# A decoder layer on one core: one wait on the load queue, another PSUM bank for two weight transposes, and five re-ordered steps of the input quantisation

## The reference, cut to what matters

```python
x = x + attention(layernorm(x))                  # own keys, softmax over keys, two cells masked to -1e9
x = x + cross_attention(layernorm(x), ctx, mask) # K, V from ctx; softmax(energy, axis=1): over the HEADS
x = x + ffn(layernorm(x))                        # gate, up (256->1024), down (1024->256)

def fake_quant_nvfp4(x, global_scale):           # per block of 16: e4m3 scale, e2m1 values
    amax = max(abs(xb), axis=-1)
    sc8  = clip(amax / 6 * global_scale, 0, 448).astype(e4m3)
    dq   = sc8 / global_scale
    a    = clip(abs(xb) / dq, 0, 6)
    q    = sign(xb) * FP4_VALS[digitize(a, FP4_MIDS)]
    return q * dq
```

## Time and profile before

| | us |
|---|---|
| median of three runs | 632.37 |
| the profiled execution | 634.35 |
| its span in the trace | 632.3 |
| self attention, and the change of block | about 0 to 170 |
| cross attention, passes 0 to 15 | about 177 to 505 |
| feed-forward loop | about 505 to 632 |

### The profile page before, as it was taken

The page is one execution under the profiler, slowest core; times in us unless marked ns, Lnnn a source line. Parts: engine busy times, 40 slices in busy tenths (PEclk is TensorE's granted clock), DMA queues, the critical chain, the costliest instruction groups (busy, mean ns, idle before and its releaser), DMA issues.

```text
span 632.3 us, 14568 instructions
## 1 busy us (share of the span) xinstructions
PE 522.1 (83%) x6000; PEld 378.5 (60%) x6000; DVE 519.0 (82%) x660; ACT 332.9 (53%) x563; POOL 359.3 (57%) x295
## 2 busy tenths in 40 slices
PE   4799999997488999999999998998999664645544
PEld 4677777775356777767676676666776432323332
DVE  3587888888666788788899898888899889999996
ACT  2566766664153655556664575456554442625332
POOL 6401332232315776768858868777867768585540
PEclk9899999999697999999999999999999795778766
DMA  8900000000010011101111011101100000000000
GB/s 200 302 36 2 2 2 3 2 2 2 9 58 6 2 43 43 39 11 41 43 43 34 11 43 43 45 3 42 45 8 9 1 9 7 4 14 18 17 33 33
DMA packets 16644, 20.75 MB, mean 33 GB/s; under 512 B 2822, under 2 KB 14323, under 8 KB 16579
## 3 DMA queue, kind: packets, MB, share of 16 engines
q1 hardware_dynamic: 14658, 19.04, 10.0%
q10 hardware_dynamic: 1920, 0.79, 0.6%
HBM read 16.16 MB, written 1.84 MB: 28 GB/s over the span
## 4 chain that ended last, share of the span: by engine, by line
DVE 30%; PE 25%; POOL 12%; issue 4%; ACT 1%; DVEq 0%; POOLq 0%
DVE negmax L796 11%; POOL work L1214 6%; PE scores L1339 5%; PE head_out L1377 5%; PE scores L1349 4%; DVE den L804 4%; PE wide L1441 3%; DVE x_r L862 2%; DVE rden L809 2%; PE head_out L1365 2%; DVE work L903 1%; PE small L1463 1%; DVE unit L890 1%; POOL qv L1271 1%; DVE work L899 1%
## 5 line engine op out<-in xcount | busy, mean ns | idle before, releaser
L1214 POOL TENSOR_TENSOR work<-work,rden 125x1792 f32<-125x1792 f32 x48 | 172.3, 3589 | 3.8
L1040 ACT ACTIVATE work<-scores 125x896 f32<-125x896 f32 x96 | 88.7, 980 | 99.5 <-PE scores L1349 98.2
L796 DVE TENSOR_REDUCE negmax<-scores 125x112 bf16<-125x1792 f32 x48 | 97.2, 2025 | 33.5 <-PE scores L1339 33.0
L804 DVE TENSOR_REDUCE den<-work 125x56 f32<-125x896 f32 x96 | 101.9, 1062 | 10.3 <-ACT work L1040 9.9
L1212 POOL TENSOR_TENSOR rden<-rden,stays 125x112 f32<-125x112 f32 x48 | 20.5, 427 | 89.7 <-DVE rden L809 89.7
L1349 PE MATMUL scores<-negmax,identb 125*125 125x448 bf16 x192 | 46.5, 364 | 18.1 <-DVE negmax L796 15.6
L311 DVE TENSOR_REDUCE a_mpad<-a_s_ps 112x8 bf16<-112x896 f32 x32 | 33.5, 1093 | 24.3 <-PE a_s_ps L485 21.2
L1339 PE MATMUL scores<-qz,kT 32*125 32x224 f32 x768 | 51.2, 382 | 1.2 <-DVE gateT L791 0.8
L1377 PE MATMUL head_out<-work,v 125*32 125x112 f32 x1536 | 49.9, 270 | 2.1 <-POOL work L1214 2.1
L1441 PE MATMUL wide<-ctxT,ck 128*128 128x375 f32 x128 | 49.7, 513 | 0.0
L1506 PE MATMUL wide<-identb,qv 128*128 128x128 bf16 x112 | 14.1, 304 | 42.2 <-POOL qv L1271 34.5
(11 more groups left out here) (220 smaller groups left out, 1207.5 us busy)
## 6 DMA issues: line engine op xcount, KB each, us to landing
ctx_sb<-in_ctx SPq DMA_DIRECT2D x16, 375.0 KB
mask_sb<-in_mask_Bx1xSxS_if SPq DMA_DIRECT2D x16, 164.1 KB, 5.5
xsx<-in_x SPq DMA_DIRECT2D x4, 448.0 KB, 9.1
out_x<-ores SPq DMA_DIRECT2D x6, 256.0 KB, 2.1
a_raw_w<-in_L_ffn_gate_w SPq DMA_DIRECT2D x1, 1024.0 KB, 6.2
a_raw_w<-in_L_ffn_up_w SPq DMA_DIRECT2D x1, 1024.0 KB, 8.7
a_raw_w<-in_L_ffn_down_w SPq DMA_DIRECT2D x1, 1024.0 KB, 10.7
xt<-xsx SPq DMA_DIRECT2D x4, 112.0 KB, 2.2
```

Source lines behind the costliest of these rows:

```text
L796: dve.tensor_reduce(negmax[0:KP, :], scores[0:KP, :, 0:4 * TOK].rearrange("p j (h t) -> p t j h", h=4), AX.XY, ALU.max, negate=True).then_ ...
L804: link(dve.tensor_reduce(den[0:KP, kc, half], ex2[0:KP, kc, :, half, :].rearrange("p g t s -> p t g s"), AX.XY, ALU.add))
L1040: act.activation(ex2[0:KP, kc, 4 * i:4 * i + 4].rearrange("p (j m) t s -> p j m s t", m=NE), scores[0:KP, 2 * i:2 * i + 2, 0:4 * TOK].rear ...
L1214: pool.tensor_tensor(ex2[0:KP, kc], ex2[0:KP, kc], over, ALU.mult).then_inc(s["prob"], 1)
```

## The change

On the load queue of the first block a wait for the first of the `max` counts is put ahead of the first context load:

```diff
+                sp.wait_ge(s["max"], 1)
                 for b in range(2):
                     load_context(sp, b, b)
                     load_mask(sp, b, b)
```

The third weight half goes through `small` instead of `head_out`, and the halves 2 to 5 are spread over passes 0 to 3, one each, all at the place that halves 3 to 5 had. VectorE copies them at the place that halves 2 and 3 had:

```diff
-            return (scores[:, 0], head_out[:], head_out[:], small[:], small[:], small[:])[i].bitcast(BF16)
+            return (scores[:, 0], head_out[:], small[:], small[:], small[:], small[:])[i].bitcast(BF16)
...
-                        if b == 0:
-                            pe.wait_ge(s["w_sb"], 3)
+                        if b == 0:
+                            pe.wait_ge(s["w_sb"], 2)
...
                 def weight_T(i):
-                    if i == 2:
-                        pe.wait_ge(s["w_sb"], 2)
-                        pe.wait_ge(s["gone_read"], 2)
-                    if i >= 3:
+                    if i >= 2:
                         small_free()
                         pieces_read.n = i + 1
...
                         key(new, 0, 0)
-                    if n == 0:
-                        weight_T(2)
                     if now:
                         score(now, 2)
...
                         key(new, 1, 1)
-                    if n == 0:
-                        weight_T(3)
-                    if n in (1, 2):
-                        weight_T(n + 3)
+                    if 0 <= n < 4:
+                        weight_T(n + 2)
```

On VectorE `x_shifted` moves from behind `key_max` of chunk 1 to behind `inverse` of chunk 2 of the old batch, and `x_inverse` from behind `key_max` of chunk 1 to behind `x_variance`, near the end of the pass:

```diff
                     if old:
                         head_sum(old, 2, 1)
                         inverse(old, 2)
+                    if fourth is not None:
+                        x_shifted(fourth)
...
                         x_block_max(second)
-                    if third is not None:
-                        x_inverse(third)
-                    if fourth is not None:
-                        x_shifted(fourth)
                     if now:
                         head_sum(now, 0, 1)
                         inverse(now, 0)
                         head_sum(now, 1, 0)
                         key_max(now, 2)
-                    if n == 0:
-                        weight_piece(2)
-                        weight_piece(3)
-                    if n in (1, 2):
-                        weight_piece(n + 3)
+                    if 0 <= n < 4:
+                        weight_piece(n + 2)
                     if first is not None:
                         x_statistics(first)
                         x_variance(first)
+                    if third is not None:
+                        x_inverse(third)
                     if fourth is not None:
                         x_rounded(fourth)
```

On ScalarE `x_magnitude` moves from the middle of one pass to the start of the next, and for pair 4 behind the second input copy of the feed-forward part:

```diff
-                    second, third = pair_begun(n - 1), pair_begun(n - 2)
+                    second, fourth = pair_begun(n - 1), pair_begun(n - 3)
+                    if fourth is not None:
+                        x_magnitude(fourth)
                     if now:
                         half_exp(now, 0, 0)
...
                         flat_values(now)
-                    if third is not None:
-                        x_magnitude(third)
...
                 input_T_copy(1)
+                x_magnitude(NPT - 3)
```

On GpSimd `x_scales` moves behind `normalise` of chunk 2 of the old batch, and `x_units` behind `own_queries` and `output_bias`:

```diff
                     if earliest is not None:
                         x_product(earliest)
-                    if earlier is not None:
-                        x_scales(earlier)
                     if old:
                         normalise(old, 2)
                     if earlier is not None:
-                        x_units(earlier)
+                        x_scales(earlier)
                     if now:
                         normalise(now, 0)
                     if new:
                         own_queries(new)
                         output_bias(new)
+                    if earlier is not None:
+                        x_units(earlier)
                     if now:
                         normalise(now, 1)
```

## The result

The changed kernel took 625.14 us (median of 4 runs, 621.93 to 627.40), the kernel before, run beside it, 633.12 us (4 runs, 630.69 to 634.58). The ratio is 0.9865 with an interval of 0.9821 to 0.9909. The profiled execution took 627.4 us, of which the trace spans 625.5; before it was 634.35 and 632.3.

What follows compares the result with a forecast made beforehand. No single engine bounds it: PE and DVE are both busy 82 to 83%, and cross attention is a ring of dependent steps. 5.5 - 0.1 + 2.06 + 1.55 + 0.45 = 9.5 us off 632.37 gives 622.9 us; range 619.5 to 628.

Steps and rivals of the forecast that it cites:

- The weight strand: Pass 0: mask-copy wait and one weight transposition removed from before the scores of chunk 2; 5.5 us gained.
- The copy from pass 1: Pass 0's new timing taken from the same sequence in pass 1: scores of pass 1 at 194.85 instead of 200.35.
- The rival of a slow clock: Pass 0: PE stays at the lower clock, so 5.5 us becomes 2.8; time 625.6 us, chance 0.13.
- The weight half in pass 3: Pass 3 gets one transposition and a copy it did not have; cost 0.1 us, at most 1.01.
- The context loads: Four load DMAs wait 1.7 us for the first maximum; taken as 0, at most 0.5 us gain or loss.
- The GpSimd order: Passes 8, 10, 15: seven small POOL operations no longer precede normalise(old, 2); PE's waits for L1214 go, 2.06 us gained.
- x_shifted: Moved right behind the inverse, with POOL idle, taking 0.68 us: 1.55 us off passes 8, 10, 15, and 0.45 after pass 11.
- x_inverse: This 0.34 us DVE step moves to a place with 0.3 to 0.4 us of idle DVE time; cost 0.
- nothing comes of it: ScalarE or the query operand replaces pass 0's wait and the rest cancels: 631 to 633 us, chance 0.04.
- only the weight strand pays: x_shifted and the GpSimd order change who waits, not when a pass ends: 627.0 us, chance 0.13.
- `x_shifted` loses the race: Passes 7, 9, 11, 14: POOL issues first and DVE stands until L1214 ends; slower, 638.2 us, chance 0.04.
- PE stays fast at the end of pass 15: Clock stays high there: 0.7 us for head outputs and 0.6 for scores gained on top; 621.6 us, chance 0.13.

Runs made afterwards that it cites:

- the experiment that keeps the wait: Changed kernel with TensorE's wait for ScalarE's mask copy put back ahead of the scores of chunk 2 in pass 0, without the transposition: 631.01 us.
- the kernel of the input steps alone: Kernel before with only the order of the quantisation steps changed, without the load wait and the weight transposes' edits: 629.65 us, ratio 0.9949.
- the later comparison: Unaltered changed kernel timed again, beside the one with x_shift behind the last half sum of chunk 2: 625.23 us, ratio 0.9871; the other 621.65 us, 0.9818.

## Why the prediction was right, and where it was not

*The weight strand: right, in place and size.* Forecast 5.5 us, measured 5.53. That the two meet so closely is in part luck: against the three executions with the old order it is 4.2 to 5.6. The copy from pass 1 carried over to the instruction: from the scores of chunk 2 to those of pass 1 it said 5.95 us, and it is 5.99 (191.15 to 197.14). PE stands still for 0.69 us, where 0.7 was said. The rival of a slow clock (2.8 us, not 5.5) falls; the experiment that keeps the wait shows that its mechanism is real, and comes with the wait: 2.65 us of idle time, and then 1.64 us lost at a low clock.

*The weight half in pass 3: right.* 0.1 forecast, 0.10 measured.

*The context loads: right as far as it can be told.* The kernel with that edit alone shows no change, in an interval from 0.6 us faster to 2.6 us slower; the 0.5 us that were allowed can't be tested by it. The 2.3 us by which pass 0 began later in the profiled execution are not from it. Ten profiled executions with the wait begin pass 0 at 174.1 to 179.8 us, four without it at 174.3 to 180.0, and the changed kernel alone at 179.68 and 174.06.

*The GpSimd order: nearly right.* All three waits of PE for POOL are gone. The kernel with `x_shifted` at its old place against the kernel before shows -0.48 and -0.67 us for passes 7 to 10 and -0.64 for 14 and 15: 1.8 us, of the 2.06 forecast. The missing part sits in passes 7, 9 and 14, which grew by 0.27, 0.09 and 0.11 in that kernel; the paragraph on `x_inverse` says why. `x_magnitude` at 0 was right: in pass 11 it takes 0.62 us, and ScalarE still stands idle for 4.10 us behind it.

*x_shifted: right in sum, wrong in place.* Forecast 1.55 + 0.45 = 2.0 us, measured 2.0. L857 takes 0.63 us, where I took 0.68. The row that I read for it was not one with POOL idle: L1263 of POOL began at 518.37, just behind L856 at 518.35, and took 2.45 us. But I had the late start of passes 8, 10 and 15 shrink from 1.09 to 0.6 us. It vanished, and passes 7, 9 and 14 became 0.6 to 0.8 us longer instead. The prediction said itself that the maximum of chunk 1 would come 0.6 us later, and took that as hidden. It is, alone: where `x_shift` doesn't wait, passes 7, 9 and 14 are 19.6 us long with `x_shifted` at the new place. It is not on top of the wait of 0.81 us that `x_shift` puts ahead of the same maximum. The prediction never named that wait. It said that DVE has no idle time in passes 7, 9 and 14, and that reading was wrong: the trace of before has DVE idle there for 0.54, 0.68 and 0.62 us ahead of `x_shift`. In passes 11 and 12 the gain was 0.68 instead of 0.45 us, which hid part of what was missing elsewhere.

*x_inverse: wrong at 0.* I put it at 0 because it moved to a place with 0.3 to 0.4 us of idle DVE time. That place is ahead of the inverse for which GpSimd waits, GpSimd's normalisation stands ahead of `x_deviation`, and VectorE asks for `x_deviation` at the start of the next pass with nothing left to do meanwhile. In the kernel with only `x_shifted` put back passes 7, 9 and 14 came out 0.27, 0.09 and 0.11 us longer, 0.47 in all, and 0.36 of it came back in the kernel with `x_inverse` ahead of `key_max` of chunk 2: 0.14 of the 0.27 in pass 7, where the other 0.13 lies in `x_variance`, held up beside GpSimd. The rest of the 1.0 us that this kernel gains lies in passes 6, 8, 10, 11 and 13, in which the changed kernel lost nothing by the move of `x_inverse` (pass 6 is 19.64 and pass 11 19.96 us, before 19.62 and 19.96): it is a gain that the forecast did not claim, and no part of its shortfall.

*The shortfall.* Passes 7 to 15 gave 3.5 us of the 4.1 forecast in the profiled execution. In three more kernels in which these passes have the same order they gave 3.9, 3.9 and 3.2, and 3.0 in the second profiled execution of the changed kernel. The spread comes from the end of pass 15, where the clock differs.

*The rivals.* That nothing comes of it falls with the interval of the result, which ends at 0.9909. That only the weight strand pays (627.0) falls with the kernel of the input steps alone, 0.9949 with an interval below 1. That `x_shifted` loses the race doesn't happen at this place. One half sum later it does: passes 7 to 12, 14 and 15 of that kernel are 13.9 us longer than before, where the working, with GpSimd's gain of 2.06 taken off, had 11.2; it left out the clock behind the wait. Its time of 638.2 us met a measured 640.0. PE stays fast at the end of pass 15: not in the changed kernel (1.72 us), but in two of its variants, for 0.8 us instead of the 1.3 allowed, and for 0.4 to 1.2 us against the other executions with the same steps. Which of the two comes in a given execution no run settles.

*The rest.* Between the first and the last score group the change gave 8.9 us of the 9.5 forecast. By the medians it gave 8.0 us (633.12 to 625.14) and, in the later comparison, 8.8 (634.04 to 625.23). The forecast of 622.9 us had been counted from 632.37, the median of the first three runs; 0.8 of the 2.2 us between it and 625.14 is that the runs beside the changed kernel had a median of 633.12.

## What to carry to other kernels

When a step is moved into a gap of its own engine, follow the next result of that engine which another one waits for, and on to where that one's answer is wanted back: a gap ahead of a handover is not free. A step that waits for another engine should have one step of its own engine put ahead of it; here this, one half sum, was worth about as much as the move of the five steps (3.9 us against 3.5 by the passes, 3.6 against 3.2 by the medians and ratios). And a long wait of TensorE is priced with the slow instructions behind it, where the clock falls: here these came to 1.5 and 1.6 us on top of 3.1 and 2.0.

## What the runs showed of the hardware

*The start of pass 0 scatters by 6 us,* from 174.1 to 180.0, and by 5.6 us between two executions of the changed kernel itself, 179.68 and 174.06. It goes with TensorE's granted clock early on. The stretch from 22 to 35 us of the two executions, first that with the late start; the third figure from the end is the clock:

```profile
22.00:35.00 13.00, 11.15 (x125) 8.80 (x123) 6.21 (x13) 6.90 (x19) 3.01 (x4) 0.74 0.81 250
```

```profile
22.00:35.00 13.00, 10.87 (x174) 8.40 (x167) 11.18 (x19) 6.83 (x17) 3.66 (x5) 1.00 0.76 242
```

TensorE did 174 matrix multiplications in the one and 125 in the other in the same time, and VectorE had 11.18 us of work instead of 6.21. Over all fourteen profiled executions it is the same: with a granted clock of 1.00 in this stretch pass 0 began at 174.1 to 176.1 us (five), with 0.87 at 175.1 to 177.4 (three, the kernel before among them), with 0.74 at 178.8 to 180.0 (six). What decides it, no run here tells; it is why a single profiled execution can't price an edit of 2 us by its span, and the passes had to be compared one by one.

*The blocking grows with what is left of the other engine's instruction.* The same `x_shifted` took 0.63 us free, 1.20 us with 0.66 us of POOL's product still to run, and 3.73 us with 3.18 still to run: both times it ended about 0.55 us after the product did.

The Trainium skill, page "SBUF — State Buffer", section "Who interferes with whom", has a VectorE instruction with two SBUF inputs and a GpSimd instruction that reads SBUF contend for an exclusive lock, and the order of issue decide which of them is blocked. The trace agrees both ways: with GpSimd first `x_shifted` took 3.73 us, and with VectorE first (L857 at 322.02) GpSimd's L1211 took 0.74 us instead of 0.42.

*The same wait, either clock.* In pass 15 PE stood still for 1.89 us ahead of a subtraction in every execution with the new order. The head outputs behind it took 1.69 to 1.72 us in nine of them and 1.01 in two, the kernels with `x_inverse` one step earlier and with `x_shifted` one half sum later. The length of the wait alone doesn't decide the clock.
